# Loading the next batch's x in four pieces, splitting it on GpSimd alone, and giving the third head group early lower projections

## The reference, cut to what matters

```python
q = split_heads(x @ Wq.T + bq)
k = split_heads(x @ Wk.T + bk)
v = split_heads(x @ Wv.T + bv)
q_lr = einsum('bhtd,hdr->bhtr', q, Wq_lsr)
k_lr = einsum('bhtd,hdr->bhtr', k, Wk_lsr)
attn = softmax(where(causal, q_lr @ k_lr.T / sqrt(32), -inf))
y = (attn @ v) @ Wo.T + bo
x = layernorm(x + y)
```

## Time and profile before

| | us |
|---|---|
| median of three runs | 3893.7 (3890.47 to 3897.09) |
| the profiled execution | 3893.05 |
| its span, first to last instruction | 3891.3 |
| TensorE busy | 3630.7 (93%) |
| VectorE busy | 2260.8 (58%) |
| ScalarE busy | 1488.4 (38%) |
| GpSimd busy | 666.7 (17%) |
| mean granted clock of TensorE | 0.956 |

### The profile page before, as it was taken

The page is one execution under the profiler, slowest core; times in us unless marked ns, Lnnn a source line. Parts: engine busy times, 40 slices in busy tenths (PEclk is TensorE's granted clock), DMA queues, the critical chain, the costliest instruction groups (busy, mean ns, idle before and its releaser), DMA issues. The chain is left out here.

```text
span 3891.3 us, 55460 instructions
## 1 busy us (share of the span) xinstructions
PE 3630.7 (93%) x19935; PEld 2505.5 (64%) x19935; DVE 2260.8 (58%) x4972; ACT 1488.4 (38%) x2793; POOL 666.7 (17%) x859
## 2 busy tenths in 40 slices
PE   4899999999999999999999737999999999999995
PEld 3555556556555555565555337888888888888884
DVE  2576665675765766657657475444444444544456
ACT  1253443443444434434434322333333333333335
POOL 2022121121121221211211201011111111111113
PEclk8999999999999999999999855999999999999997
DMA  5234234233323252332332203343343343444448
GB/s 169 61 93 127 76 92 123 62 97 112 102 72 113 79 142 64 101 110 71 89 115 66 72 0 99 100 139 117 112 131 111 120 124 111 130 121 117 143 157 308
DMA packets 207200, 423.14 MB, mean 109 GB/s; under 512 B 45840, under 2 KB 48912, under 8 KB 198800
## 3 DMA queue, kind: packets, MB, share of 16 engines
q1 hardware_dynamic: 180304, 367.47, 30.6%
q0 software_dynamic: 14400, 35.14, 4.6%
q10 hardware_dynamic: 12288, 17.83, 1.7%
HBM read 246.23 MB, written 72.38 MB: 82 GB/s over the span
## 5 line engine op out<-in xcount | busy, mean ns | idle before, releaser
L833 ACT ACTIVATE probs<-scores_t 128x512 f32<-128x512 f32 (+3 forms) x1536 | 656.8, 496 | 574.6 <-PE scores_t L700 516.9
L1801 PE MATMUL m_ps_h<-m_tokens_t,m_w_parts 128*128 128x512 f32 x3072 | 739.7, 391 | 1.6 <-DVE m_tokens_t L1683 1.6
L1801 PE MATMUL m_ps_y<-m_w_parts,m_hidden_parts 128*128 128x512 f32 x3072 | 737.3, 390 | 0.6
L1801 PEld LDWEIGHTS m_ps_y<-m_w_parts,m_hidden_parts 128*128 128x128 f32 x3072 | 575.3, 188 | 125.8 <-issue 6.3
L1801 PEld LDWEIGHTS m_ps_h<-m_tokens_t,m_w_parts 128*128 128x128 f32 x3072 | 575.3, 188 | 120.1 <-issue 2.0
L889 DVE CUSTOM_DVE_ANT_0 shared_banks<-shared_banks,mask_q_rows 128x128 f32<-128x128 f32 (+3 forms) x1024 | 477.7, 515 | 176.4 <-PE shared_banks L657 173.9
L657 PE MATMUL shared_banks<-k_operands,q_operands 96*128 96x512 f32 (+3 forms) x1536 | 509.3, 379 | 23.7 <-DVE natural L880 8.9
L700 PE MATMUL scores_t<-q_operands,k_operands 128*128 128x512 f32 (+3 forms) x1536 | 494.7, 372 | 33.3 <-ACT probs L833 26.1
L1619 ACT ACTIVATE m_hidden<-m_ps_h,m_b 128x512 f32<-128x512 f32 x256 | 176.6, 690 | 791.1 <-PE m_ps_h L1801 777.9
L562 POOL TENSOR_SCALAR_AFFINE_SELECT probs<-probs 128x256 f32<-128x256 f32 x512 | 220.3, 433 | 1341.3 <-ACT probs L833 1340.7
L657 PEld LDWEIGHTS shared_banks<-k_operands,q_operands 96*128 96x128 f32 x1536 | 279.0, 191 | 263.7 <-issue 122.9
(11 more groups left out here) (243 smaller groups left out, 3225.2 us busy)
## 6 DMA issues: line engine op xcount, KB each, us to landing
m_w_raw<-in_w1T SPq DMA_DIRECT2D x64, 1024.0 KB, 5.2
m_w_raw<-in_w2T SPq DMA_DIRECT2D x64, 1024.0 KB, 7.5
wqk_group<-scratch_wqk SPq DMA_DIRECT2D x32, 1024.0 KB, 5.6
q_operands<-natural SPq DMA_DIRECT2D x192, 128.0 KB, 2.6
k_operands<-natural SPq DMA_DIRECT2D x192, 128.0 KB, 2.7
q_operands<-natural SPq DMA_DIRECT2D x384, 64.0 KB, 2.0
k_operands<-natural SPq DMA_DIRECT2D x384, 64.0 KB, 2.0
natural<-in_xT SPq DMA_DIRECT2D x8, 2048.0 KB, 9.8
```

The costliest lines, as they stand in the source:

```text
L833: act.activation(probs[:, slot_of(k, h // 2), h % 2, c0:HALF], st[:, (HG * k + h) % SCORE_BANKS, c0:HALF], ACT.Exp, scale=SCALE).then_inc( ...
L1801: mm = pe.matmul(bank, a, b, start=(first and n == 0), stop=(final and n == len(pairs) - 1))
```

## The change

`load_x` loads 32 rows of x of each of the four chunks (512 KB) for one head number h. It waits only for that head's upper strips of slot 1, and for the lower strips of its pair. In slot 1's `strips` the load of piece h-1 is issued behind the six strips of head h, the last piece behind all; the weights of group 0 follow after it. `x_in` counts 64 for a batch. The lead-in loads its x in the same four pieces, one issue after the other.

ScalarE waits for x, and copies the first part, behind (5, 2); the other three behind (6, 0), (6, 2) and (7, 0). GpSimd makes all four rests, queued behind the masks of step 3 (`X_LO_AT = 3`), so ahead of those of step 8; VectorE makes none.

`HALVED` is 3: the third slot has its lower projections at 41 and 44 and early lower strips, and its `strips` copy upper halves only. The fourth slot takes its maxima and its reciprocals in the order of the other slots; the head-by-head order is left to the lead-in alone.

```diff
-def max_steps(g):
+def max_steps(by_head):
...
-    if g < GROUPS - 1:
+    if not by_head:
         return sum(lower, []) + sum(upper, [])
     return sum((lower[h] + upper[h] for h in range(HG)), [])
...
-HALVED = 2
+HALVED = 3
...
-MAX_EARLY = (1, 1, 0, 2, 0, 2, 2, 1, 0, 0, 2, 1, 0, 0, 0, 3, 0, 0, 1, 1,
+MAX_AFTER = (1, 1, 0, 2, 0, 2, 2, 1, 0, 0, 2, 1, 0, 0, 0, 3, 0, 0, 1, 1,
              1, 1, 1, 0, 2, 0, 1, 1, 2, 0, 2, 0, 1, 2, 0, 1, 1, 2, 1, 2,
              1, 1, 0, 1, 0, 1, 1, 1, 2, 0, 2, 0, 0, 0, 0, 0, 0, 0, 0, 0)
-MAX_LATE = (0, 0, 0, 0, 0, 0, 0, 0, 0, 2, 2, 1, 1, 0, 3, 0, 0, 0, 3, 0,
...
-MAX_AFTER = (MAX_EARLY,) * 3 + (MAX_LATE,)
-PROJ_AFTER = ((27, 42, 56, 57),) * HALVED + ((46, 47, 56, 57),) * 2
+PROJ_AFTER = ((27, 42, 56, 57),) * 2 + ((41, 44, 56, 57), (46, 47, 56, 57))
...
-X_HI_AT = ((7, 0), (7, 2), (8, 0), (8, 2))
-X_LO_POOL = 2
-X_LO_AT = 6
-X_LO_DVE_AT = (8, 3)
-INVERT_AFTER = ((((30, 36, 42, 45), (2, 6, 10, 14)),) * 3 + (((30, 42, 45, 45), (0, 4, 4, 5)),))
+X_HI_AT = ((5, 2), (6, 0), (6, 2), (7, 0))
+X_LO_POOL = DC
+X_LO_AT = 3
+INVERT_AFTER = ((30, 36, 42, 45), (2, 6, 10, 14))
...
-            def load_x(b, n):
-
-                for h in range(HG):
-                    sp.wait_ge(strips_sent[h], n * STRIPS)
-                for half in lower_sent:
-                    sp.wait_ge(half, n // GROUPS * HALVED * LOWER_STRIPS)
-                sp.dma_start(nat[:], xT_dram.rearrange("(c p) t -> p c t", p=P)[:, :, bass.ds(b * T, T)]
+            def load_x(b, h):
+
+                rows = slice(DH * h, DH * h + DH)
+                sp.wait_ge(strips_sent[h], b * GROUPS * STRIPS)
+                sp.wait_ge(lower_sent[h // 2], (b * HALVED - 1) * LOWER_STRIPS)
+                sp.dma_start(nat[rows], xT_dram.rearrange("(c p) t -> p c t", p=P)[rows, :, bass.ds(b * T, T)]
                              ).then_inc(x_in, 16)
...
-            def strips(b, slot, lead=False, heads=range(HG), first=0, weights=None):
+            def strips(b, slot, lead=False, heads=range(HG), first=0, weights=None, x_of=None):
...
+                    if x_of is not None and h > 0:
+                        load_x(x_of, h - 1)
+                if x_of is not None:
+                    load_x(x_of, HG - 1)
...
-                for slot in range(HALVED):
-                    lower_strips(b, slot)
-                    early = slot + 1 < HALVED
-                    strips(b, slot, first=HALF, weights=(slot + AHEAD + 1) % GROUPS if early else None)
-                    if more and not early:
-                        load_w((slot + AHEAD + 1) % GROUPS)
+                lower_strips(b, 0)
+                strips(b, 0, first=HALF, weights=GROUPS - 1)
+                lower_strips(b, 1)
+                strips(b, 1, first=HALF, x_of=b + 1 if more else None)
                 if more:
-                    load_x(b + 1, b * GROUPS + GROUPS)
-                    strips(b, GROUPS - 2)
+                    load_w(0)
+                    lower_strips(b, 2)
+                    strips(b, 2, first=HALF)
                     load_w(1)
...
-            load_x(0, 0)
+            for h in range(HG):
+                rows = slice(DH * h, DH * h + DH)
+                sp.dma_start(nat[rows], xT_dram.rearrange("(c p) t -> p c t", p=P)[rows, :, 0:T]).then_inc(x_in, 16)
...
                     ins = pool.tensor_tensor(xs[:, LO, c, :], nat[:, c, :], raw(xs[:, HI, c, :]), ALU.subtract)
-                ins.then_inc(x_split, 1)
+                ins.then_inc(x_split, 2)
...
                             if item[2:] == X_HI_AT[0]:
-                                act.wait_ge(x_in, 16 * (b + 2))
+                                act.wait_ge(x_in, 16 * HG * (b + 2))
...
-                    if kind == "scores" and b < NB - 1 and item[1] == GROUPS - AHEAD and item[2:] == X_LO_DVE_AT:
-                        for c in range(X_LO_POOL, DC):
-                            dve.wait_ge(x_hi, DC * b + c + 1)
-                            ins = dve.tensor_tensor(xs[:, LO, c, :], nat[:, c, :], raw(xs[:, HI, c, :]), ALU.subtract)
-                        ins.then_inc(x_split, 1)
```

More of the change, by code:

```diff
@@ L198 @@
 AHEAD = 2
-MAX_EARLY = (1, 1, 0, 2, 0, 2, 2, 1, 0, 0, 2, 1, 0, 0, 0, 3, 0, 0, 1, 1,
+MAX_AFTER = (1, 1, 0, 2, 0, 2, 2, 1, 0, 0, 2, 1, 0, 0, 0, 3, 0, 0, 1, 1,
              1, 1, 1, 0, 2, 0, 1, 1, 2, 0, 2, 0, 1, 2, 0, 1, 1, 2, 1, 2,
              1, 1, 0, 1, 0, 1, 1, 1, 2, 0, 2, 0, 0, 0, 0, 0, 0, 0, 0, 0)
-MAX_LATE = (0, 0, 0, 0, 0, 0, 0, 0, 0, 2, 2, 1, 1, 0, 3, 0, 0, 0, 3, 0,
-            2, 0, 3, 1, 0, 0, 2, 0, 1, 2, 0, 1, 2, 1, 2, 0, 0, 2, 1, 1,
-            0, 2, 2, 4, 1, 0, 1, 2, 1, 0, 1, 1, 0, 0, 0, 0, 0, 0, 0, 0)
-MAX_AFTER = (MAX_EARLY,) * 3 + (MAX_LATE,)
-PROJ_AFTER = ((27, 42, 56, 57),) * HALVED + ((46, 47, 56, 57),) * 2
+PROJ_AFTER = ((27, 42, 56, 57),) * 2 + ((41, 44, 56, 57), (46, 47, 56, 57))
 LOWER_READ_AT = (3, 7)
@@ L237, in plan_slot @@
         order += [("proj", g, i) for i, at in enumerate(PROJ_AFTER[g]) if at == n]
-        order += [("invert", g, 0, i) for i, at in enumerate(INVERT_AFTER[g][0]) if at == n]
+        order += [("invert", g, 0, i) for i, at in enumerate(INVERT_AFTER[0]) if at == n]
         if g > 0:
-            order += [("invert", g - 1, 1, i) for i, at in enumerate(INVERT_AFTER[g][1]) if at == n]
-        order += [("max", g, i) for i in range(done, done + MAX_AFTER[g][n])]
-        done += MAX_AFTER[g][n]
+            order += [("invert", g - 1, 1, i) for i, at in enumerate(INVERT_AFTER[1]) if at == n]
+        order += [("max", g, i) for i in range(done, done + MAX_AFTER[n])]
+        done += MAX_AFTER[n]
         if n == JOIN_AFTER:
@@ L356, in build_attention @@
         LOWER_STRIPS = STRIPS * HG // 2
-        steps, maxes = attend_steps(), [max_steps(g) for g in range(GROUPS)]
+        steps, halves_first, by_head = attend_steps(), max_steps(False), max_steps(True)
         NE = len(steps)
@@ L650, in run @@
                     elif kind == "max":
-                        g, (h, _, it, k0, n) = item[1], maxes[item[1]][item[2]]
+                        g, (h, _, it, k0, n) = item[1], (by_head if lead else halves_first)[item[2]]
                         if it == 0 and not lead and 1 <= g <= HALVED and h % 2 == 0:
@@ L834, in exps @@
                                ACT.Exp, scale=SCALE).then_inc(exp_done, 1)
-            act.wait_ge(x_in, 16)
+            act.wait_ge(x_in, 16 * HG)
             for c in range(DC):
@@ L884, in run @@
                     elif kind == "max":
-                        h, slot, it, k0, n = maxes[item[1]][item[2]]
+                        h, slot, it, k0, n = (by_head if lead else halves_first)[item[2]]
                         dve.wait_ge(bank_full[bank], off[bank] + turn + 1)
```

## The result

The changed kernel takes 3926.6 us (median of 4 runs, 3922.96 to 3928.82) against 3893.7: the ratio is 1.0084, 95% interval 1.0066 to 1.0101. **It is 33 us slower.** The forecast was 3904 with a range of 3881 to 3922: the side was right, the size was a third of it, and the time lies outside the range.

What follows compares the result with a forecast made beforehand. The prediction took the tensor engine as the bound, busy 3630.7 of 3891.3 us. Third slots +20, fourth slots -14 and lead-in +5 made +11 on the profiled 3893: 3904 us, range 3881 to 3922.

Steps and rivals of the forecast that it cites:

- (a): Third slot, x in four pieces: last piece issued at 18.9, landing at 24.0, with 2.5 us of data per piece.
- (b): Third slot, copies at (5,2) to (7,0): score (6,2) 6.2 us late instead of 2.8; with 2.6 behind it, +20 us.
- Behind the wait: Third slot, loss after the late score (6,2), half clock expected again: 2.6 us, near the earlier 3.1.
- upper end of 5.2: Third slot, highest loss behind the wait: another 3.4 us half-clock stretch, +1.7, on batch 1's 3.5.
- more half clock: Rival, chance 0.1: one more half-clock stretch per third slot, pieces at half rate, 7 x 2.6 more, 3922 us.
- lower end: Third slot, lowest loss behind the wait: 1.4 us, half the half-clock stretch falling while TensorE stands idle.
- Mostly half clock: Third slot of the kernel before: the 3.1 us lost behind the standing, with ScalarE's four copies crowded between exponentials.
- (c): Third slot, all subtractions on GpSimd: 0 to 0.5 us wait before the projection at 41, taken as 0.
- (d): Third slot, weights after the pieces, projections at 41 and 44: weights hidden, lower strips landed by 56, in time.
- (e): Fourth slot in the early order: 52.1 to 50.1 us, 7 x -2.0 = -14, bounds -8 and -15.
- (f): Lead-in, x in four pieces landing in 12.1 us instead of 7.2: +5 us, bounds 0 and 6.
- the prediction's own formula: Whole change: 7(X-21.1)-14 plus the lead-in, where X is the last piece's landing in the third slot.

Runs made afterwards that it cites:

- e9: The changed kernel with the same four narrow pieces of x all issued behind the last strip of slot 1: 3945.4 us.
- e5: The changed kernel with x whole again, one load of 128 partitions behind all strips, in the lead-in too: 3910.5 us.
- e1: The kernel before with only ScalarE's copies of x moved to (5,2), (6,0), (6,2), (7,0): 3941.6 us.
- e10: The changed kernel with 30 extra matmuls ahead of score (6,2) in the third slots of batches 0 to 6: 3925.1 us.
- e6: The changed kernel with copies back at (7,0) to (8,2) and the third group's lower projections at 46 and 47: 3886.6 us.
- e7: The kernel before with whole x ahead of the weights, the third group's early lower strips (projections at 46, 47) and the fourth slot's early order: 3858.3 us.
- e8: The changed kernel with x in two 128-partition loads, a semaphore each; copies from (7,0), subtractions shared with VectorE, third group's lower projections at 44 and 46: 3844.7 us.
- e3: The kernel before with x, still one load, issued ahead of the weights of group 0 instead of behind them: 3870.7 us.
- e4: The kernel before with only the lead-in's load of x in four pieces of 32 partitions: 3896.9 us.
- e2: The kernel before with the batches' x in four pieces between the strips and the weights behind; lead-in and copies as before: 3874.9 us.

## Why the prediction was wrong

Point by point, against the terms of its sum (20 - 14 + 5 = +11 against a measured +29.9 in the profiled executions).

**(a) The landing: the step that failed.** The prediction put the last piece's issue at 18.9 and its landing at 24.0; they were 20.3 and 26.0. Two things were missed. First, I counted for the strips only the issues that stand ahead of them, and left their landing at 2.0 us. Behind a piece it is near 4 (e9 takes the pieces away from between them and it is 2.0 again), and the last piece waits for it: 1.4 us. Second, the last piece took 5.7 us from issue to landing in the mean, not 5.1 (4.2 for a piece alone, and the rest behind piece 2): 0.6 us. The median of all 28 is 5.4. The rate was right: 2.5 us of data for a piece, as the strips suggested.

The Trainium skill (SBUF — State Buffer, Door 1: The DMA port swizzle) gives about 218 GB/s for partitions 0 to 31, from which the prediction had an estimated 2.4 us; the landings of e9 agree within 0.1 us.

So it is the time around the data that was too short. The lead-in's first piece, with no strip about, already takes 5.0 us (the least of its four; the others queue behind it):

```profile
DMA to landing us min/median/max: 5.0/8.2/11.2
```

Why it is 5.0 and not 4.2 no run tells. Both misses add to 2.0 us a batch, **14 of the 19 us** by which the sum fell short. The range was made from bounds of one piece on its own (3.3 to 4.2 us) and allowed the landing one microsecond more; the second microsecond of error had no place in it.

**(b) The place of the copies: right, and the heart of it.** The blocked score starts 1.6 us behind the landing and is measured from 19.4: 27.6 - 19.4 = 8.2 late in the mean, batch 1's 7.9 in the rows above. (The 19.4 is the first of the pair at 530.49, not the second, as the prediction has it; its value is right.) Over e5, the changed kernel and e9 the third slot grows by 4.2 us while the landing moves by 3.8 (25.2, 26.0, 29.0 to 60.5, 61.4, 64.7): what lands later is paid for nearly one for one. e1 shows the place alone at +50 us.

**Behind the wait**, I took 2.6 us; it was 11.3 - 8.2 = 3.1, the size it had before: another 0.5 x 7 = 3.5 us. Here a wait was put at nothing. In each of the seven third slots a maximum matmul stands 0.58 us for VectorE's part of a projection's results, 4.1 us in all, seven of the eleven waits in the second row (the first is of the kernel before, which has one such wait of 0.3 us in these seven batches):

```profile
PE shared_banks L657 <- DVE natural L880: 8.9, 5, 4.8
...
PE shared_banks L656 <- DVE natural L874: 13.7, 11, 5.9
```

The kernels with the projections at 41 and 44 have it (e5, e9, e10), those at 46 and 47 or 44 and 46 do not (e6, e7, e8). The upper end of 5.2 did not come about, although in five of seven slots the clock was down for 10.2 us, one stretch more than before, as the rival "more half clock" had it: about half of that fell into TensorE's standing, the part for which I had made the lower end.

How much of the 3.1 is the clock's? In the changed kernel some 1.6, for 1.5 are left at full clock (e10), 0.6 of them the wait above. For the kernel before it is shown only in part: in the six slots of e3 at full clock 2.0 of its 3.1 are still there, 0.7 of them the wait for the last subtraction. "Mostly half clock" was thus too simple for before; how the 3.1 us there divide between clock and split was not measured apart.

**(c) All subtractions on GpSimd: right as the sum has it.** No wait of a projection for GpSimd stands among the changed kernel's. The cover was as thin as worked out, and held by what came late for other reasons: take the half clock away (e10) and the projection starts 0.1 us behind the last subtraction; put the copies and projections later (e6) and it waits for GpSimd, 18.0 us in all.

**(d), (e) Early lower strips and the fourth slot: right.** -14 forecast, -13.4 measured; the strips were in time. e7 gives -12.4 for this part on another kernel.

**(f) The lead-in: right.** +5 forecast, +5.4 in the profiled execution, +5.7 by itself (e4). Its wait in the changed kernel, to be set beside the earlier trace rows:

```profile
60.40 2.05 PE L687 MATMUL shared_banks<-x_parts,wqk_group 128*128 128x512 f32 x4 [23.79 <-DVE x_parts L943]
```

With 26.0 and 3.1 in the prediction's own formula the sum is 11 + 14 + 3.5 = +28.5, against +29.9. The side of the forecast was no luck, since the place of the copies makes it; its size was short by the landing.

The changed kernel's median lies 33 us above the old one, 3 more than the two profiled executions; its profiled execution was the quickest of its four.

## What to carry to other kernels

A wait for a transfer has a place in the queue of the engine that waits, and moving the work behind it forward moves the wait forward as well: here the load came 1.8 us sooner, and what it held up was wanted 7.2 us sooner. When loads are squeezed between other DMAs of a queue, price what they do to those that follow, above all if the last load waits for one of these. Cutting a load can help where each consumer waits for its own part (e8, where other things moved too); it did not where all wait for the last (e2 against e3, the changed kernel against e5).

## What the runs showed of the hardware that was not expected

- A 64 KB copy that landed in 2.0 us took 3.7 to 4.1 behind a 512 KB load into 32 partitions in the same queue, and 2.0 again when the loads stood behind it (e9).
- 210 more instructions of TensorE in the attention (e10) made the experts' stage, 500 us and more behind the last of them, some 9 us longer: 12 gaps of up to 1.3 us ahead of the experts' matmuls that the profile puts down to nothing but "issue", and 177 packets of instruction fetches in queue 8, where the changed kernel and all others here have 121. That the longer program lies differently for the loop of the experts is a guess; it was not tried apart.
- The granted clock fell in none of the seven third slots when TensorE had 7 us of matmuls to do in its 8 us of waiting (e10), and in all seven when it had none (mean clocks of 0.92 and 0.94).
